# Fields of a factorization layer kept once, in every tenth column of the products' buffer

## The reference

```python
def _cin_layer(X, prev_x, W, b):
    x_i = jnp.einsum('bmd,bhd->bmhd', X, prev_x).reshape(bsz, m * h, d)
    return jnp.einsum('oc,bcd->bod', W, x_i) + b[None, :, None]

e = jnp.stack([tbl_0[ids[:, 0]], ..., tbl_31[ids[:, 31]]], axis=1)   # (512, 32, 64)
prev_x, outs = e, []
for W, b in ((W0, b0), (W1, b1)):              # W0 (128, 1024), W1 (128, 4096)
    x_i = _cin_layer(e, prev_x, W, b)
    outs.append(x_i.sum(axis=2))
    prev_x = x_i
h = jnp.concatenate([jnp.concatenate(outs, axis=1), dense_ctx], axis=1)
h = jnp.maximum(h @ W_top1 + b_top1, 0.0)
h = jnp.maximum(h @ W_top2 + b_top2, 0.0)
y = h @ W_top3
```

## Time and profile before

| | |
|---|---|
| median of 3 runs | 196.04 us (195.92 to 197.17) |
| span of the profiled execution | 194.2 us, from its first to its last instruction; 1.8 us less than the median, which lies outside the span |
| TensorE | 181.0 us busy (93%) |
| ScalarE | 144.9 us busy (75%) |
| VectorE | 137.3 us busy (71%) |
| GpSimd | 123.8 us busy (64%) |

### The profile page before, as it was taken

The page is one execution under the profiler, slowest core; times in us unless marked ns, Lnnn a source line. Parts: engine busy times, 40 slices in busy tenths (PEclk is TensorE's granted clock), DMA queues, the critical chain, the costliest instruction groups (busy, mean ns, idle before and its releaser), DMA issues.

```text
span 194.2 us, 8803 instructions
## 1 busy us (share of the span) xinstructions
PE 181.0 (93%) x3815; PEld 157.7 (81%) x3815; DVE 137.3 (71%) x307; ACT 144.9 (75%) x349; POOL 123.8 (64%) x134
## 2 busy tenths in 40 slices
PE   6999999869669959999999999989999999999985
PEld 6999999749557738878898877868888879889984
DVE  2007799994499999999996499977765796693100
ACT  2499977549848997899868879979677797776333
POOL 3777787877777777777777777777777777000000
PEclk9999999999999997999999999999999999999999
DMA  6991111111123334427211411331141114010100
GB/s 182 311 339 33 27 29 24 29 25 30 27 51 64 84 83 75 118 54 177 50 30 30 81 30 30 50 58 30 32 83 32 30 32 75 17 23 14 29 3 0
DMA packets 16520, 12.26 MB, mean 63 GB/s; under 512 B 12513, under 2 KB 12897, under 8 KB 16482
## 3 DMA queue, kind: packets, MB, share of 16 engines
q1 hardware_dynamic: 12242, 7.44, 15.1%
q0 software_dynamic: 4096, 4.20, 11.2%
q10 hardware_dynamic: 144, 0.07, 0.1%
HBM read 9.59 MB, written 0.00 MB: 49 GB/s over the span
## 4 chain that ended last, share of the span: by engine, by line
POOL 47%; PE 31%; issue 16%; DMA 3%; ACT 2%; DVE 0%; ACTq 0%
POOL rows L626 47%; PE psum L458 13%; PE psum L220 7%; PE psum L545 3%; PE psum L527 3%; DMA rows<-table,idx 2%; PE psum L480 2%; PE psum L516 2%; PE psum L190 1%; DMA t_sb<-ids 1%; ACT t_sb L261 1%; PE psum L562 1%; DVE acc_sb L465 0%; ACT acc_sb L731 0%; ACT xx L271 0%
## 5 line engine op out<-in xcount | busy, mean ns | idle before, releaser
L626 POOL DMA_INDIRECT rows<-table,idx x128 | 123.1, 962 | 40.8 <-issue 38.7
L288 DVE TENSOR_TENSOR prod<-psum,xx 128x256 f32<-128x256 f32 (+3 forms) x160 | 85.7, 603 | 22.2 <-ACT xx L271 12.0
L261 ACT ACTIVATE t_sb<-psum 64x308 f32<-64x308 f32 (+1 forms) x180 | 76.4, 425 | 10.2 <-PE psum L205 3.9
L458 PE MATMUL psum<-coef,t_sb 128*64 128x128 f32 (+1 forms) x954 | 53.7, 275 | 0.0
L458 PEld LDWEIGHTS psum<-coef,t_sb 128*64 128x64 f32 (+1 forms) x954 | 47.4, 131 | 4.3 <-issue 4.1
L220 PE MATMUL psum<-prod,xx 64*32 64x154 f32 x1920 | 42.4, 300 | 2.0 <-ACT coef L731 0.9
L257 DVE COPY t_sb<-psum 64x308 f32<-64x308 f32 x64 | 30.8, 481 | 10.8 <-PE psum L220 9.5
L220 PEld LDWEIGHTS psum<-prod,xx 64*32 64x32 f32 x1920 | 30.7, 107 | 9.4 <-issue 5.9
L271 ACT ACTIVATE xx<-psum 128x256 f32<-128x256 f32 x32 | 12.3, 386 | 11.0 <-PE psum L190 10.6
L190 PE MATMUL psum<-ident,rows 128*128 128x128 f32 x64 | 13.6, 295 | 3.1 <-DVE prod L288 2.0
L358 DVE TENSOR_TENSOR t_sb<-t_sb,coef 128x64 f32<-128x64 f32 (+8 forms) x63 | 15.8, 321 | 0.2
(11 more groups left out here) (39 smaller groups left out, 120.9 us busy)
## 6 DMA issues: line engine op xcount, KB each, us to landing
rows<-table,idx POOLq DMA_INDIRECT x128, 2.7
t_sb<-t_sb SPq DMA_DIRECT2D x28, 64.0 KB
w_sb<-w1t SPq DMA_DIRECT2D x3, 512.0 KB, 6.9
t_sb<-w0x SPq DMA_DIRECT2D x1, 768.0 KB, 10.3
w0g_sb<-w0g SPq DMA_DIRECT2D x1, 512.0 KB, 9.2
w_sb<-top SPq DMA_DIRECT2D x2, 256.0 KB
w_sb<-top SPq DMA_DIRECT2D x1, 512.0 KB
w_sb<-w1t SPq DMA_DIRECT2D x1, 384.0 KB, 4.7
```

Source lines behind the costliest of these rows:

```text
L261: copy_t(act, lambda o, i: act.activation(o, i, ACT.Copy), 0, u, v)
L288: return dve.tensor_tensor(at(p, col, out), at(psum, XT[g] * BANK + a, first), at(x, x0 + b, second), ALU.mult)
L458: return pe.matmul(bank(ACC, half * O, O, j, width), t_sb[:, c:c + width], w, start=i < places, stop=i >= n - places, tile_position=(0, j))
L626: pool.indirect_dma_start(rows[:, c:c + D], None, table[:, :], bass.IndirectOffsetOnAxis(ap=idx[:, g:g + 1], axis=0))\
```

## The change

The buffers `xx` are gone. ScalarE copies the 256 numbers of a half once, from PSUM straight into `prod`, each into every tenth column (`copy_fields`). The blocks of `prod` get a pitch of 80 columns, of which 77 are used, so that the step of 10 runs on through all 32 blocks. These fields serve three uses: as weights of the groups (read with a step of 10), as gram columns, and as the second factor of the products (read with a step of 10). The products are spread between them: OUTER and INNER are written with a step of 2 columns, SQUARE and NEXT in runs, and the far pairs with a step of 4. The semaphores `xx_ready` and `gram_ready` become one, `fields_ready`. The columns of `t_sb` follow the new order (`T_COL`), and `pack` reads every fourth column.

```diff
+STEP = 10
+PITCH = STEP * GRAM
+AT_FAR, AT_FIELD, AT_OUTER, AT_INNER, AT_SQUARE, AT_NEXT, AT_ONE = 0, 1, 3, 43, 63, 72, 76
...
-        prod = [sb(f"prod{n}", SUB // 2 * 4 * COLS) for n in range(4)]
-        xx = [sb(f"xx{n}", SUB * M) for n in range(2)]
+        prod = [sb(f"prod{n}", SUB // 2 * 4 * PITCH) for n in range(4)]
...
+        def fields_of(p, j, r):
+
+            return at(p, 4 * j * PITCH + AT_FIELD, [[STEP, M]], D * r, D)
...
         def wide_group(pe, u, v):
...
                             last = pe.matmul(bank(TG + 2 * (v % 2) + r, 2 * n * COLS, 2 * COLS, 32 * (2 * i + k), M),
-                                             xx[u % 2][D * r:D * (r + 1), x:x + M],
-                                             p[D * r:D * (r + 1), y + 2 * k * COLS:y + 2 * (k + 1) * COLS],
+                                             fields_of(p, j, r),
+                                             at(p, (4 * j + 2 * k) * PITCH, [[PITCH, 2], [1, COLS]], D * r, D),
                                              start=True, stop=True)
...
-        def act_xx(act, u, g):
+        def copy_fields(act, u, g):
 
             act.wait_ge(xt_done, 2 * u + g + 1)
             wait(act, t_done, 4 * (u - 2) + 2 * (g + 1))
-            x0 = g * SUB // 2 * M
-            act.activation(xx[u % 2][:, x0:x0 + SUB // 2 * M], bank(XT[g], 0, SUB // 2 * M), ACT.Copy).then_inc(xx_ready, 1)
-
-        def act_gram(act, u, g):
-
-            act.wait_ge(xx_ready, 2 * u + g + 1)
-            wait(act, t_done, 4 * (u - 2) + 2 * (g + 1))
-            src = at(xx[u % 2], g * SUB // 2 * M, [[GRAM, 2 * SUB], [1, GRAM]])
-            dst = at(prod[2 * (u % 2) + g], PAIRS, [[COLS, 2 * SUB], [1, GRAM]])
-            act.activation(dst, src, ACT.Copy).then_inc(gram_ready, 1)
+            act.activation(at(prod[2 * (u % 2) + g], AT_FIELD, [[STEP, SUB // 2 * M]]), bank(XT[g], 0, SUB // 2 * M), ACT.Copy)\
+                .then_inc(fields_ready, 1)
...
             def pairs(col, out, first, a, second, b):
-                return dve.tensor_tensor(at(p, col, out), at(psum, XT[g] * BANK + a, first), at(x, x0 + b, second), ALU.mult)
-
-            pairs(OUTER, [[COLS, 2 * SUB], [4, 4], [1, 4]], [[QUART, 2 * SUB], [1, 4], [0, 4]], 0,
+                return dve.tensor_tensor(at(p, col, out), at(psum, XT[g] * BANK + a, first),
+                                         at(p, AT_FIELD + b * STEP, [[STEP * d, n] for d, n in second]), ALU.mult)
+
+            pairs(AT_OUTER, [[PITCH, 2 * SUB], [STEP, 4], [2, 4]], [[QUART, 2 * SUB], [1, 4], [0, 4]], 0,
                   [[QUART, 2 * SUB], [0, 4], [1, 4]], 4)
...
-            pairs(NEAR, [[COLS, 2 * SUB], [1, 2 * FAR]], [[HALF, SUB], [1, QUART], [0, QUART]], 0,
+            pairs(AT_FAR, [[PITCH, 2 * SUB], [2, 2], [4, FAR]], [[HALF, SUB], [1, QUART], [0, QUART]], 0,
                   [[HALF, SUB], [0, QUART], [1, QUART]], QUART).then_inc(prod_ready, 1)
...
-        T_COL = [*range(NEAR), COLS - 1, *range(NEAR, NEAR + FAR)]
+        T_COL = [AT_OUTER + STEP * a + 2 * b for a in range(4) for b in range(4)]
+        T_COL += [AT_INNER + STEP * m + 2 * n for m in range(2) for n in range(4)]
+        T_COL += [AT_SQUARE + n for n in range(QUART)] + [AT_NEXT + n for n in range(4)] + [AT_ONE]
+        T_COL += [AT_FAR + 4 * n for n in range(FAR)]
```

More of the change, by code:

```diff
@@ L131, in build @@
         xt_done = sem("xt_done")
-        xx_ready = sem("xx_ready")
-        gram_ready = sem("gram_ready")
+        fields_ready = sem("fields_ready")
         prod_ready = sem("prod_ready")
@@ L185, in transpose_rows @@
             pe.wait_ge(gathered[u % UNITS][g], 16 * TILES // 2 * (u // UNITS + 1))
-            for ready in (xx_ready, prod_ready):
+            for ready in (fields_ready, prod_ready):
                 wait(pe, ready, 2 * (u - 1) + g + 1)
@@ L228, in t_group @@
             if v % 2 == 0:
-                pe.wait_ge(gram_ready, 2 * u + v // 2 + 1)
+                pe.wait_ge(fields_ready, 2 * u + v // 2 + 1)
                 pe.wait_ge(prod_ready, 2 * u + v // 2 + 1)
@@ L281, in products @@
         def products(dve, u, g):
-            p, x, x0 = prod[2 * (u % 2) + g], xx[u % 2], g * SUB // 2 * M
+            p = prod[2 * (u % 2) + g]
             dve.wait_ge(xt_done, 2 * u + g + 1)
-            dve.wait_ge(xx_ready, 2 * u + g + 1)
+            dve.wait_ge(fields_ready, 2 * u + g + 1)
             wait(dve, t_done, 4 * (u - 2) + 2 * (g + 1))
             def pairs(col, out, first, a, second, b):
-                return dve.tensor_tensor(at(p, col, out), at(psum, XT[g] * BANK + a, first), at(x, x0 + b, second), ALU.mult)
@@ L293, in products @@
                   [[QUART, 2 * SUB], [4, 2], [0, 2], [1, 2]], 2)
[L294 to L297 removed]
+            pairs(AT_SQUARE, [[PITCH, 2 * SUB], [1, QUART]], [[1, 2 * SUB * QUART]], 0, [[1, 2 * SUB * QUART]], 0)
@@ L298, in products @@
+            pairs(AT_NEXT, [[PITCH, 2 * SUB], [1, 4]], [[QUART, 2 * SUB], [2, 4]], 0, [[QUART, 2 * SUB], [2, 4]], 1)
+            pairs(AT_FAR, [[PITCH, 2 * SUB], [2, 2], [4, FAR]], [[HALF, SUB], [1, QUART], [0, QUART]], 0,
                   [[HALF, SUB], [0, QUART], [1, QUART]], QUART).then_inc(prod_ready, 1)
@@ L736, in _ @@
                 if n == 9:
-                    act_xx(act, 0, 0)
-                    act_gram(act, 0, 0)
+                    copy_fields(act, 0, 0)
                 copy_pairs(act, n)
-            act_xx(act, 0, 1)
-            act_gram(act, 0, 1)
+            copy_fields(act, 0, 1)
             for n in range(FIRST, len(SLOTS)):
                 if n in (FIRST + 7, FIRST + 11):
-                    act_xx(act, 1, (FIRST + 7, FIRST + 11).index(n))
-                    act_gram(act, 1, (FIRST + 7, FIRST + 11).index(n))
+                    copy_fields(act, 1, (FIRST + 7, FIRST + 11).index(n))
                 copy_cross(act, n)
@@ L753, in _ @@
                 if n == 10:
-                    act_xx(act, 2, 0)
-                    act_gram(act, 2, 0)
+                    copy_fields(act, 2, 0)
             act.wait_ge(bias_ready, 1)
@@ L762, in fields_in @@
             def fields_in(u, g):
-                act_xx(act, u, g)
-                act_gram(act, u, g)
-            act_xx(act, 2, 1)
+                copy_fields(act, u, g)
+            copy_fields(act, 2, 1)
             copies(1, 0)
-            act_gram(act, 2, 1)
             copies(1, 1)
@@ L833, in _ @@
             for n in range(8):
-                last = dve.memset(at(prod[n // 2], COLS * (1 + SUB * (n % 2)) - 1, [[COLS, SUB]]), 1.0)
+                last = dve.memset(at(prod[n // 2], PITCH * SUB * (n % 2) + AT_ONE, [[PITCH, SUB]]), 1.0)
             last.then_inc(fills_ready, 1)
```

23 lines of the change are left out of this document (9 added, 14 removed).

## The result

The changed kernel takes 227.53 us (median of 6 runs, 226.61 to 229.63) against 196.6 us (195.76 to 197.61, 6 runs) of the kernel before, run beside it: ratio 1.158, 95% interval 1.153 to 1.163. The prediction was 223 us with a range of 195 to 248. The profiled execution took 226.97 us, of which 225.2 are its span.

What follows compares the result with a forecast made beforehand. VectorE's beat bounds the middle, TensorE with the last gathers the later part. Unit 2's products end at 65.7, plus 136.8 for 26 halves, 2 for gaps, 17.0 to the end, 1.8 for the median: 223 us, range 195 to 248.

Steps and rivals of the forecast that it cites:

- The removal: ScalarE loses 32 `act_gram` instructions, 14.0 us, beside other engines' work: worth nothing by itself, at most 0.5 us.
- The copy of the fields: ScalarE's single copy into every tenth column: 628 ns against 386 + 438; products wait 0.2 us longer for it.
- VectorE's price: Stepped elements in VectorE's products cost 1.75 ns instead of 1.04, over 2176 elements: 1.54 us per half.
- one path only: Rivals: only stepped writes pay (200 to 206 us) or only TensorE's weight loads (200 to 215); put at 205, chance 0.13.
- Two beats: Rival: each stepped element costs VectorE 2.08 ns, 2.27 us per half; 245 us, range 238 to 250, chance 0.27.
- free steps: Rival: VectorE takes stepped elements at its own rate, 1.04 ns; 196 us (195 to 197), chance 0.24.
- Weight loads: TensorE's 64 stepped loads per half, 0.98 us, might double: 0 to 0.98 us per half, up to 5 us in the range.
- first copy of the loop (end of unit 2's products): VectorE's coefficient copies end at 57.3 us; unit 2's products take 8.4 more, to 65.7 (61.03 before).
- 26 halves without waits: VectorE's products after unit 2: 26 halves at 3.72 + 1.54 = 5.26 us, 136.8 us, to 202.5.
- VectorE's waits in TensorE's long gaps: Five of 15 later gaps exceeded 5.26 us, by 3.9 us in all; 2 us counted, to 204.5.
- from the last products to the last groups: Last groups follow the products' end at 204.5 us without added delay; the packing DMAs were set to nothing.
- from there to the end: From the last half's groups on TensorE to the end of the span: 17.0 us, unchanged from the kernel before.

Runs made afterwards that it cites:

- Experiment 1: Kernel before with ScalarE's second copy, into the gram columns, left out from unit 2 on: 196.66 us, ratio 1.002.
- experiment 5: Changed kernel with OUTER's and INNER's factor loops exchanged and the far pairs in four instructions of 256, written two columns apart: 203.14 us, ratio 1.034.
- experiment 4: Kernel before with single 256-element instructions at varied steps behind its last work; VectorE products took 424 ns at step 2, 599 at 10; run time no verdict.
- experiment 2: Changed kernel with contiguous xx back as the products' second factor, then copied into every tenth column; stepped product writes stay: 209.3 us, ratio 1.066.
- experiment 6: Changed kernel with loops exchanged, far pairs in four instructions, and the squares written by ScalarE from PSUM instead of VectorE: 198.94 us, ratio 1.009.

## Why the prediction was right, and where it was off

The direction, the mechanism and the engine were right, and the time lies in the forecast's own range of 216 to 230, 4.5 us above the value given. Point by point:

- **The removal** was counted at nothing. Experiment 1 shows it: 1.002.
- **The copy of the fields** was put at 628 ns; it takes 650.
- **VectorE's price** was put at 1.54 us per half; it is 1.61 by the forms. The far pairs were put at 1.94 us and take 2.06. The price of an element, 1.75, is right (1.72 alone in experiment 4), and so is the reading of the fills in the earlier trace rows, which took it from the spacing of their starts. But the price was charged to every element alike, where it depends on the order of visits. SQUARE pays in full (601 − 414 = 187 ns by experiment 5, 182 charged), and so does OUTER (386, 364 charged). NEXT pays more (124, 91 charged): its step is 20, and 124 / 128 = 0.97 ns on top agrees with 0.99 by line 945. INNER, if SQUARE took the 601 ns of experiment 5 here too, took 2 × 541 − 601 = 481 and pays 67 ns where 182 were charged, and the far pairs pay 846 where 727 were. These last two misses, 115 ns too much and 119 too little, cancel by luck. Why INNER pays so little, and why the far pairs pay 0.83 ns per element where line 952 pays (609 − 424) / 256 = 0.72, no run shows by itself.
- **Reads and writes**: the sum took one price where both are stepped. Experiments 2 and 4 show that this is so (2051 against 2059, 613 against 599). The two "one path only" rivals fall with experiment 2, which leaves the far pairs' whole price and takes the others'.
- **Two beats** would have given 2.28 us for the far pairs; **free steps** 1.21. Neither is there. By the Trainium skill, "VectorE: DVE Perf Modes", section Mode 1× (REGULAR), the free case was to be expected; the measurement decides against it for SBUF from a step of 3 on (486 and 599 against 424). The Trainium skill, "SBUF — State Buffer", section Specifications (TRN2), asks for two hits in a line of 16 bytes: with fp32 a step of 2 gives them, 3 gives them part of the time and 4 never, and lines 938, 939 and 940 follow it. An estimate by these lines: if each new line costs 1.72 ns, four elements at a step of 3 lie in three lines, and 256 of them take 424 + 64 × (3 × 1.72 − 4 × 1.04) = 488 ns, against 486 measured.
- **Weight loads** grew by a third, 107 to 140 ns, not to double; a half's two groups take 1.35 us instead of 1.29, as at 208.14 us. TensorE waits 19.1 us for VectorE's products in all (line 191), which covers it.

The span came to 225.2 instead of 221.5 us, by these terms:

| term of the sum | forecast | measured | difference |
|---|---|---|---|
| first copy of the loop (end of unit 2's products) | 65.7 | 66.90 | +1.2 |
| 26 halves without waits | 136.8 | 138.4 | +1.6 |
| VectorE's waits in TensorE's long gaps | 2 | 1.2 | −0.8 |
| from the last products to the last groups | 0 | 1.63 | +1.6 |
| from there to the end | 17.0 | 17.06 | +0.1 |

The first is in the main a push that the prediction counted in its two-beat rival only: VectorE's copies of the coefficients (line 410) come behind its products of 45.34 us and start at 49.55 instead of 46.49, and the groups and the copies behind them follow at 54.34, where 53.2 was forecast (0.1 of this is the forecast's own rounding: from 43.61 to 45.3 it is 1.7 us, not 1.6). The second is the larger price, 1.60 us per half instead of 1.54. The third is the two waits of 0.66 and 0.56 us, for which 2 were allowed. Of the fourth, 1.30 us are the wait for the packing, whose cost the prediction set to nothing. Of the remaining 0.8 us of the 4.5, 0.5 is the median's distance from the profiled execution (227.53 against 226.97, which again lies 1.8 above its span), and 0.3 is the rounding of the forecast.

The packing starts when VectorE's last copy is done. In the changed kernel it took 4.98 us from there (202.15 to 207.13), and TensorE had reached its last part after 3.68. In the kernel before TensorE reached that part after about 4.6 us (171.72 to some 176.3) and did not wait, so the packing had taken no longer than that. So about 0.9 us of the wait come from TensorE being there sooner, and 0.4 or more from a slower packing. Experiments 2, 5 and 6, whose far pairs lie in the same columns as in the changed kernel, wait there too (0.88, 1.09 and 1.21 us). That the step of four columns is what slows it is not shown: no run has it alone.

## What to carry to other kernels

Before a layout is interleaved to save a copy, count who visits each element how often: here the copy lay on an engine with time to spare, and the step was paid on up to 2176 elements per half by the engine that set the beat. In these runs a 32-bit operand in SBUF was free of the price when its neighbours lay at most two columns away (424 ns at steps of 1 and 2), or when each place was used at least twice in a row (421 ns for the forms of experiment 6); exchanging the loops of a broadcast product bought most of it back without touching the layout. Read a fill by the spacing of its starts, not by the length of its row.

## What the hardware showed unexpectedly

- The time of a lone element is nearly the same on two engines that differ in their contiguous rate: 1.72 ns on VectorE (1.04 contiguous) and 1.77 on ScalarE (0.83).
- The row of a VectorE fill has the same length at every step (272 ns), while the starts of such fills lie 0.40 us apart at a step of 1 and 0.57 at a step of 4.
- A step of 20 columns is dearer than its neighbours (678 ns against 578 at 16 and 581 at 32; lines 945, 944 and 946 of experiment 4). Why is open.
- TensorE pays for its moving operand too: 276 ns for 128 columns at step 1, 281 at 2, 404 at 4 and 411 at 10.
- TensorE's clock fell while it waited for VectorE. Stretches of the changed kernel (columns as in the earlier trace rows), and TensorE there in order of time:

```profile
78.50:83.70 5.20, 1.74 (x59) 1.06 (x50) 5.15 (x7) 3.25 (x9) 3.98 (x5) 0.76 0.28 76
83.70:86.40 2.70, 2.70 (x72) 2.04 (x58) 2.67 (x5) 1.75 (x4) 2.07 (x3) 0.50 0.35 58
```

```profile
82.84 0.66 PE L191 MATMUL psum<-ident,rows 128*128 128x128 f32 x2 [3.46 <-DVE prod L280]
83.43 2.31 PE L220 MATMUL psum<-prod 64*32 64x154 f32 x64
```

After 3.46 us of waiting the granted clock was 0.50, the 1.2 GHz level, and a half's groups took 2.31 us instead of 1.35. VectorE's starts at 83.73 and 89.02 us stayed 5.3 apart, so it cost VectorE's beat nothing.
